# Reciprocals of an attention denominator in two row halves: packed broadcasts and sums, three parts by masks

## The reference

```python
q = jax.nn.elu(q) + 1.0
k = jax.nn.elu(k) + 1.0
q_cos, q_sin = (q * cos, q * sin)
k_cos, k_sin = (k * cos, k * sin)
...
qkv = jnp.einsum('bshx,bhxz->bshz', q_cos, kv_cos) + jnp.einsum('bshx,bhxz->bshz', q_sin, kv_sin)
denom = 1.0 / (jnp.einsum('bshd,bhd->bsh', q_cos, k_cos.sum(axis=1)) + jnp.einsum('bshd,bhd->bsh', q_sin, k_sin.sum(axis=1)) + 1e-05)
o = qkv * denom[..., None]
```

## Time and profile before

| | |
|---|---|
| median of 3 runs | 4081.96 us (4072.59 to 4082.1) |
| profiled execution | 4079.0 us, its span 4077.2 us |
| mean granted TensorE clock | 0.940 |

### The profile page before, as it was taken

The page is one execution under the profiler, slowest core; times in us unless marked ns, Lnnn a source line. Parts: engine busy times, 40 slices in busy tenths (PEclk is TensorE's granted clock), DMA queues, the critical chain, the costliest instruction groups (busy, mean ns, idle before and its releaser), DMA issues.

```text
span 4077.2 us, 52073 instructions
## 1 busy us (share of the span) xinstructions
PE 3586.0 (88%) x17556; PEld 1798.3 (44%) x17556; DVE 2994.3 (73%) x3523; ACT 1687.9 (41%) x1798; POOL 1248.6 (31%) x1327
## 2 busy tenths in 40 slices
PE   4798998989889998989889899899989898899976
PEld 2344444444544444444444445344444444544453
DVE  6878876788677876788767886778767887548823
ACT  0145533455254534445434553445435554343310
POOL 1015620176013740156201760127501572011100
PEclk8899998999999998999989999999989999899967
DMA  1000000000000001000000000000010000100045
GB/s 47 17 1 1 1 17 25 1 1 1 25 17 1 1 1 41 1 1 1 17 25 1 1 1 25 17 1 1 1 41 1 1 1 16 30 1 1 1 116 200
DMA packets 18676, 70.96 MB, mean 17 GB/s; under 512 B 8781, under 2 KB 13421, under 8 KB 13485
## 3 DMA queue, kind: packets, MB, share of 16 engines
q1 hardware_dynamic: 18365, 67.10, 5.3%
HBM read 37.26 MB, written 29.84 MB: 16 GB/s over the span
## 4 chain that ended last, share of the span: by engine, by line
issue 48%; PE 33%; DVE 8%; POOL 7%; ACT 2%; DMA 1%; SPq 1%; POOLq 0%; DVEq 0%; ACTq 0%
PE ps_D L1499 11%; POOL UA L549 4%; PE ps_E L1463 4%; PE ps_C L1488 3%; PE ps_A L1446 3%; PE ps_B L1446 3%; DVE RR L1106 2%; PE ps_E L1474 1%; DVE region L1076 1%; DVE arena L911 1%; PE ps_C L1417 1%; POOL RS L581 1%; PE ps_E L1512 1%; POOL RR L574 1%; DVE region L1085 1%
## 5 line engine op out<-in xcount | busy, mean ns | idle before, releaser
L562 POOL TENSOR_TENSOR arena<-arena,UHL 128x896 f32<-128x896 f32 x350 | 764.6, 2210 | 226.3 <-ACT UHL L695 211.6
L1499 PE MATMUL ps_D<-region,small 128*128 128x448 f32 x1792 | 785.2, 562 | 32.9 <-DVE OS L1112 32.8
L549 POOL TENSOR_TENSOR UA<-region,CS 128x128 f32<-128x128 f32 (+1 forms) x400 | 178.8, 449 | 1837.8 <-DVE region L986 795.3
L1085 DVE TENSOR_TENSOR region<-region,ps_C 128x896 f32<-128x896 f32 x448 | 485.9, 1085 | 247.9 <-PE ps_C L1488 247.9
L1499 PEld LDWEIGHTS ps_D<-region,small 128*128 128x128 f32 x1792 | 321.2, 194 | 346.7 <-issue 284.8
L734 ACT ACTIVATE EQ<-ps_B,NEG 128x896 f32<-128x896 f32 x224 | 225.6, 1007 | 480.4 <-PE ps_B L1446 480.3
L911 DVE SCALAR_TENSOR_TENSOR arena<-arena,W8C 128x896 f32<-128x896 f32 (+1 forms) x418 | 416.8, 1010 | 1.2
L1417 PE MATMUL ps_C<-region,UA 128*128 128x512 f32 (+1 forms) x800 | 382.7, 601 | 2.9 <-ACT region L627 2.9
L734 ACT ACTIVATE EQ<-ps_A,NEG 128x896 f32<-128x896 f32 x224 | 225.6, 1007 | 350.8 <-PE ps_A L1446 350.7
L695 ACT ACTIVATE UHL<-arena,W8C 128x896 f32<-128x896 f32 x350 | 361.2, 1032 | 0.0
L1052 DVE SCALAR_TENSOR_TENSOR region<-region,ps_B 128x1024 f32<-128x1024 f32 (+1 forms) x200 | 243.9, 1219 | 159.8 <-ACT region L713 156.4
(11 more groups left out here) (310 smaller groups left out, 5772.9 us busy)
## 6 DMA issues: line engine op xcount, KB each, us to landing
arena<-x SPq DMA_DIRECT2D x8, 1568.0 KB, 6.6
t_keep<-Y SPq DMA_DIRECT2D x7, 1568.0 KB, 6.8
w_keep<-region SPq DMA_DIRECT2D x7, 784.0 KB, 5.7
CST<-t_keep SPq DMA_DIRECT2D x2, 1568.0 KB, 10.0
small<-t_keep SPq DMA_DIRECT2D x2, 1568.0 KB, 12.8
plane<-w_keep SPq DMA_DIRECT2D x4, 784.0 KB, 15.9
UHL<-t_keep SPq DMA_DIRECT2D x2, 1568.0 KB, 12.3
out<-CST SPq DMA_DIRECT2D x2, 1568.0 KB, 11.7
```

Source lines behind the costliest of these rows:

```text
L562: pool.tensor_tensor(out=X[:, cut], in0=X[:, cut], in1=PRODUCT[m % 3], op=ALU.add).then_inc(pool_taps.sem, 1)
L1085: dve.tensor_tensor(out=q, in0=q, op=ALU.mult, in1=here.area(key)[:, :].rearrange("p (c n) -> p c n", c=2)[:, :, 0:PIX])\
L1499: ins = pe.matmul(here.area(key)[:, 0:PIX], MW[i][:, c, :], Q[s % 3][:, c, :], start=c == 0, stop=c == NCHUNK - 1)
```

## The change

The halves j move from 16-row groups to halves of the partitions: row 64 j + 16 m + h holds head h of pixel half j, part m; m = 3 is empty (its sum is 0, and no product reads it with a weight other than 0).

- `q_sums`: two products with 64 columns each (SEL is 128 x 64), one into PSUM rows 0 to 63, one into rows 64 to 127. Each is complete in itself.
- `q_broadcast`: four products of 64 rows, from partitions 0 to 63 for j = 0 and 64 to 127 for j = 1, in the order (0,0), (0,1), (1,0), (1,1) of (a, j). Half j goes to bank j of area C, block a to its columns 224 a on. `q_scale` reads area C by this order.
- `split`: four operations on 128 rows in place of five on 96 or 32, with multiplications by a column MASK of zeros and ones where rows were picked by partition; the wait for its own last operation falls away.
- RR, RS3, SELB and the guard have 128 rows; one `passed` more in `q_sums` and in `q_broadcast`.
- Setup: SELB by one copy from a small sum HEADROW, SEL by three additions, MASK by two reductions; VSETUP is 58 instead of 63 links.

```diff
-                    pool.tensor_copy(parts, RR[:, 1]).then_inc(gstep.sem, 1)
+                    pool.tensor_scalar(parts, RR[:, 1], MASK[:, 0:1], None, ALU.mult).then_inc(gstep.sem, 1)
                     pool.wait_ge(*gstep.at(pair, 3 * s + 1))
                     pool.tensor_tensor(out=RR[:, 2], in0=RR[:, 1], in1=parts,
                                        op=ALU.subtract).then_inc(gstep.sem, 1)
                     pool.wait_ge(*gstep.at(pair, 3 * s + 2))
                     passed(pool)
-                    pool.tensor_copy(parts[32:64], RR[32:64, 2])
-                    pool.tensor_copy(parts[64:96], RR[64:96, 2]).then_inc(gstep.sem, 1)
+                    pool.tensor_scalar(parts, RR[:, 2], MASK[:, 1:2], None, ALU.mult).then_inc(gstep.sem, 1)
                     pool.wait_ge(*gstep.at(pair, 3 * s + 3))
-                    pool.tensor_tensor(out=parts[64:96], in0=RR[64:96, 2], in1=parts[64:96],
+                    pool.tensor_tensor(out=parts, in0=RR[:, 2], in1=parts,
                                        op=ALU.subtract).then_inc(split_ready.sem, 1)
-                    pool.wait_ge(*split_ready.at(pair, s + 1))
-                    passed(pool)
...
             for m in range(3):
-                rows = slice(32 * m, 32 * m + 32)
-                for j in range(2):
-                    at = 32 * m + HEADS * j
-                    link(dve.tensor_copy(SELB[rows, j], IDN[rows, at:at + HEADS].unsqueeze(2)
-                                         .broadcast_to([32, HEADS, C])))
-                    link(dve.tensor_tensor(out=SEL[:, j, m, j, :].rearrange("p (g c h) -> p g c h", g=2, h=2),
-                                           in0=rows_of_heads[:, 0, 0:2], in1=rows_of_heads[:, 1, 0:2],
-                                           op=ALU.add))
+                link(dve.tensor_tensor(out=SEL[:, m * HEADS:(m + 1) * HEADS]
+                                       .rearrange("p (g c h) -> p g c h", g=2, h=2),
+                                       in0=rows_of_heads[:, 0, 0:2], in1=rows_of_heads[:, 1, 0:2],
+                                       op=ALU.add))
+            parts_of_rows = IDN[:, :].rearrange("p (j m h) -> p h j m", j=2, m=4)
+            link(dve.tensor_reduce(out=HEADROW[:, :], in_=parts_of_rows[:, :, :, 0:3], axis=AX.XY, op=ALU.add))
+            link(dve.tensor_copy(SELB[:, :, :], HEADROW[:, :].unsqueeze(2).broadcast_to([P, HEADS, C])))
+            for m in range(2):
+                rows = IDN[:, :].rearrange("p (j r) -> p j r", j=2)[:, :, (m + 1) * HEADS:3 * HEADS]
+                link(dve.tensor_reduce(out=MASK[:, m:m + 1], in_=rows, axis=AX.XY, op=ALU.add))
...
                 key = ("rb", s, cc)
-                q = Q[s % 3][:, 2 * cc:2 * cc + 2, :]
+                q = Q[s % 3][:, 2 * cc:2 * cc + 2, :].rearrange("p c (j n) -> p c j n", j=2)
+                rows = here.area(key)[:, :].rearrange("p (j n) -> p j n", j=2)[:, :, 0:PIX]
                 dve.wait_ge(*here.filled(key))
-                dve.tensor_tensor(out=q, in0=q, op=ALU.mult,
-                                  in1=here.area(key)[:, :].rearrange("p (c n) -> p c n", c=2)[:, :, 0:PIX])\
-                    .then_inc(*here.empty(key))
+                dve.tensor_tensor(out=q, in0=q, in1=rows.rearrange("p j (c n) -> p c j n", c=2),
+                                  op=ALU.mult).then_inc(*here.empty(key))
...
                 pe.wait_ge(*here.room(key))
+                passed(pe)
                 for j in range(2):
-                    ins = pe.matmul(here.area(key)[0:96, 0:SUB],
-                                    SEL[:, j].rearrange("p m d h -> p (m d h)"),
-                                    DS[:, j * SUB:(j + 1) * SUB], start=j == 0, stop=j == 1)
+                    ins = pe.matmul(here.area(key)[HALVES[j], 0:SUB], SEL[:, :],
+                                    DS[:, j * SUB:(j + 1) * SUB], start=True, stop=True)
...
-                for a in range(2):
-                    c = 2 * cc + a
-                    for j in range(2):
-                        at = a * 512 + j * SUB
-                        ins = pe.matmul(here.area(key)[:, at:at + SUB],
-                                        SELB[:, j, 2 * c:2 * c + 2, :].rearrange("p h c -> p (h c)"),
-                                        RS3[:, s % 2], start=True, stop=True)
+                passed(pe)
+                for a, j in ((0, 0), (0, 1), (1, 0), (1, 1)):
+                    c, at = 2 * cc + a, j * 512 + a * SUB
+                    ins = pe.matmul(here.area(key)[:, at:at + SUB],
+                                    SELB[HALVES[j], 2 * c:2 * c + 2, :].rearrange("p h c -> p (h c)"),
+                                    RS3[HALVES[j], s % 2], start=True, stop=True)
```

16 lines of the change are left out of this document (9 added, 7 removed).

## The result

| | before | after |
|---|---|---|
| median | 4080.3 us (4 runs, 4072.6 to 4082.1) | 4140.7 us (4 runs, 4136.9 to 4141.0) |
| profiled span, mean clock | 4077.2 us, 0.940 | 4138.8 us, 0.931 |

The changed kernel is slower: ratio 1.0151, 95% interval 1.0140 to 1.0163, some 60 us.

A forecast was written before the change was run, and what follows sets the result against it. Bound by PE, nearly full in the query stage, and by its waits for POOL's split chain. PE -1, POOL -18 and setup -3.4 sum to -22.4 us: 4079.0 becomes 4056.6, as a median 4059.5; range 4040 to 4095.

The forecast's parts named there:

- term 2, POOL: POOL's split chain, four operations for five: -0.24 us per chain, fewer PE waits, together -18 us.
- The masked multiply: POOL's TENSOR_SCALAR in `split`: taken as 0.45 us, between a CAST's 0.37 and TENSOR_TENSOR's 0.61.
- rival 3: POOL's masked multiply dearer than TENSOR_TENSOR: each 0.1 us costs 10 us, slower from 0.72, 4100 at 0.9; chance 0.10.
- The semaphore instruction: On PE, now between the wait and the broadcast's weights: put at 0.05 us, between 0 and 0.1.
- Term 1: PE's packed broadcasts and sums in the query stage: -0.01 us a step of 4 slots, -1 us over 112 steps.
- rival 4: Row halves on PE don't run beside each other: 128 us more, less 22, about 4188 us; chance 0.05.
- the limit of 0.43 us by four loads: PE broadcast: by the skill's LDWEIGHTS rule four weight loads take 0.43 us, so it could not get shorter.
- One sign: On PE in the fourth slot of a step, a full-size product follows 0.51 us behind the broadcasts' start, before 0.38.
- slot D: Fourth slot of a query step on PE, a broadcast and `q_output`: forecast 0.51 us for 0.38, so +0.13.
- A, B, C and D: A step's four slots: broadcast, then `q_denominators`; with `q_sums`; with `q_fold` in odd steps, then `q_output`; with `q_output`.
- The 0.57 us that the packing was said to save: Product time on PE saved per step by packing; seven new changes of tiling were said to take it back.
- Term 3: DVE's setup operations for SELB and SEL: 5.56 us become 2.1, so -3.4 us.

The follow-up runs named there:

- after_wait: The changed kernel with the two removed lines back behind the split's last subtraction (POOL's wait for its own result, semaphore instruction): 4071.1 us, ratio 0.9960.
- tt_mask: The changed kernel with both masked multiplies of the split as TENSOR_TENSOR with the mask column broadcast, instead of TENSOR_SCALAR: 4072.4 us, ratio 0.9978.
- tt_wait_filled_np: The changed kernel with TENSOR_TENSOR masked multiplies, the split's wait restored, unread filling products on PE and no `passed(pe)` in `q_broadcast`: 4038.1 us, ratio 0.9914.

## Why the prediction was wrong

Forecast 4059.5, range 4040 to 4095; measured 4140.7, outside it and on the other side of the kernel before. **The step that failed is term 2, POOL**, in two places:

- **What the change removes.** Term 2 prices what stands inside POOL's chain; the two lines behind the chain, POOL's wait for its own last result, have no term, not even "at nothing, because". They held POOL's tap sums 0.38 us back, and that let DVE's half-size piece in between two of them. Against after_wait, which differs by these two lines alone, the change has 42 half-size pieces over 1.6 us instead of 20, PE waits for OS 75.6 us instead of 29.8, and is idle for 39.3 us more.
- **The masked multiply**, taken as 0.45 us between bounds of 0.37 and 0.61, measured 0.84: the upper bound, an operation with two inputs, was no bound. The chain from the reciprocal's end to the split's end, forecast 0.24 us shorter, became longer: the median of the 112 is 3.88 us, before 2.92. This is rival 3, and its condition came true. But its slope of 10 us for each 0.1 makes at most some 4099 of 0.84, and that is 42 us short.

Neither accounts for the loss alone. The ratios to the kernel before, by the multiply's own price (at 0.37 the masks are left out):

| | 0.84 | 0.61 | 0.37 |
|---|---|---|---|
| as the change, without the wait | 1.0151 | 0.9978 | 0.9967 |
| with the wait | 0.9960 | 0.9946 | 0.9965 |

Either edit alone takes the whole loss back, and each kernel of this table but the change lies inside the range of the prediction. By the ratios and by the medians, the removed wait costs 1.7 to 1.9% at the price of 0.84, 0.3 to 0.5% at 0.61 and 0.0 to 0.2% at 0.37. Going from 0.61 to 0.84 costs 1.7% without the wait and 0.1 to 0.4% with it. Why the two together cost more than their sum is in part the clock: tt_mask has most of the change's meetings at the port (35 long pieces, 42 there) and loses nothing, because PE is busy for 52 us less with the same products. How the longer multiply brings the lower clock about stays open.

The other terms:

- **The semaphore instruction** on PE: from the split's end to the first broadcast 0.24 us, before 0.14, and 0.13 again in tt_wait_filled_np, which leaves it out. So 0.10, not 0.05.
- **Term 1 held.** Timeline of PE in the changed kernel:

```profile
1009.94 0.35 PE L1447 MATMUL ps_B<-plane,WQL 128*128 128x448 f16 x1
1010.23 0.37 PE L1488 MATMUL ps_C<-RS,SELB 64*128 64x224 bf16 x4
1010.52 1.77 PE L1499 MATMUL ps_D<-region,small 128*128 128x448 f32 x4
1012.13 0.35 PE L1447 MATMUL ps_A<-plane,WQH 128*128 128x448 f16 x1
```

  The broadcast starts 0.10 later than 0.19 behind its forerunner would be (1010.13), and from there the slot takes 2.00 us until the next projection: 0.51 and four products at 0.37, as forecast. Halves do run beside each other (the four products start at 0, 3, 106 and 109 ns), so rival 4 is out, and so is the limit of 0.43 us by four loads. One sign reads otherwise than forecast: the product behind them starts 0.29 us after them, not 0.51. From the broadcast's start slot D is as long as before (1.90 us until the next projection); what it costs more lies ahead of it. Over the slots without a wait, at full clock, A, B, C and D changed by about -0.09, -0.12, 0.00 and +0.09 us (forecast -0.07, -0.10, +0.03, +0.13), so a step by -0.11 instead of -0.01, 12 us in all. The 0.57 us that the packing was said to save in a step is by its own rows 4 x 0.19 + 0.38 = 1.14; no sum uses it.
- **Term 3**: FOLD's operation starts at 39.83 us instead of 43.47, 3.6 us earlier (forecast 3.4).
- **The clock** was not in the sum. In the third pair the part outside the query stage is busy for 6.6 us more with the same products, at 0.93 instead of 0.95; over the seven loop pairs these parts lose 32 us. That the falls settle into one pattern in the changed kernel is read from the periods; what sets the pattern is not shown.
